# The last 48 inner rows of each routed expert enter the down product as stacked rounded parts

## The reference, cut to what matters

```python
w_topk, sel = jax.lax.top_k(probs, K)          # K = 4 of E = 32 experts
buf = buf[:, :CAP]                             # CAP = 128 token slots an expert, H = 256
g = jnp.einsum('ech,ehf->ecf', buf, w_gate)    # F = 176 inner rows
u = jnp.einsum('ech,ehf->ecf', buf, w_up)
y = jnp.einsum('ecf,efh->ech', jax.nn.silu(g) * u, w_down)
```

## Time and profile before

| | |
|---|---|
| median of 3 runs | 700.69 us (700.65 to 703.05) |
| the profiled execution's own time | 701.29 us |
| its span, first to last instruction | 699.1 us |
| TensorE busy | 671.0 us (96%) |
| VectorE busy | 489.0 us (70%) |
| ScalarE busy | 424.3 us (61%) |
| GpSimd busy | 297.8 us (43%) |
| chain that ended last | PE 76%, DVE 14%, ACT 6%, issue 3% |
| granted clock of TensorE | 1.00 throughout |

### The profile page before, as it was taken

How to read it: one execution, slowest core, us unless ns; L and a number is a source line. 1 busy time by engine, 2 the same in 40 slices (tenths; PEclk the granted TensorE clock), 3 DMA queues, 4 the chain that set the end, 5 groups by cost and what they waited for, 6 DMA issues and landing times.

```text
span 699.1 us, 13847 instructions
## 1 busy us (share of the span) xinstructions
PE 671.0 (96%) x4756; PEld 581.7 (83%) x4756; DVE 489.0 (70%) x1418; ACT 424.3 (61%) x1099; POOL 297.8 (43%) x301
## 2 busy tenths in 40 slices
PE   6999999999999999999999989999989999999997
PEld 3777888888889898887787855666889999999997
DVE  6798877877877787777786886777465555644544
ACT  3766168788797878888663788888654213222221
POOL 0584154546464555542164318998334410400000
PEclk9999999999999999999999999999999999999999
DMA  8902044453535444351910000200300000000000
GB/s 329 346 1 98 1 130 121 165 166 112 168 116 165 129 152 126 101 159 59 365 79 1 1 1 2 107 1 3 121 1 1 1 1 16 2 16 1 1 16 16
DMA packets 26725, 59.43 MB, mean 85 GB/s; under 512 B 3146, under 2 KB 12748, under 8 KB 26272
## 3 DMA queue, kind: packets, MB, share of 16 engines
q1 hardware_dynamic: 23584, 50.35, 21.5%
q0 software_dynamic: 3072, 8.20, 3.6%
HBM read 48.24 MB, written 10.49 MB: 84 GB/s over the span
## 4 chain that ended last, share of the span: by engine, by line
PE 76%; DVE 14%; ACT 6%; issue 3%; POOL 1%; DMA 0%; DVEq 0%; ACTq 0%
PE bank L2253 11%; PE bank L2020 7%; PE bank L1954 6%; PE bank L2302 5%; PE bank L2011 5%; PE bank L2276 5%; PE bank L2040 4%; PE bank L1961 3%; PE bank L2031 3%; PE bank L2082 3%; PE bank L2316 2%; PE bank L2222 2%; PE bank L2206 2%; PE bank L1894 2%; PE bank L2161 2%
## 5 line engine op out<-in xcount | busy, mean ns | idle before, releaser
L1062 ACT ACTIVATE sb<-bank,sb 128x256 f32<-128x256 f32 x128 | 59.6, 471 | 40.6 <-DVE sb L1558 33.4
L1558 DVE TENSOR_REDUCE sb<-bank 128x2 f32<-128x512 f32 x64 | 43.7, 683 | 47.5 <-PE bank L2020 47.1
L1264 ACT ACTIVATE h_parts<-sb 128x256 fp32r<-128x256 f32 x56 | 23.4, 418 | 71.3 <-DVE sb L1809 43.4
L2020 PE MATMUL bank<-sb 128*128 128x256 f32 x256 | 66.2, 381 | 0.0
L1800 DVE TENSOR_TENSOR sb<-sb,bank 128x256 f32<-128x256 f32 x56 | 23.5, 419 | 58.1 <-ACT sb L1227 58.1
L2253 PE MATMUL bank<-rounded,b_hi 128*128 128x256 f32 x224 | 63.1, 282 | 0.0
L2253 PE MATMUL bank<-rounded,b_lo 128*128 128x256 f32 x224 | 62.9, 281 | 0.0
L2253 PE MATMUL bank<-am_lo,b_hi 128*128 128x256 f32 x224 | 62.9, 281 | 0.0
L1227 ACT ACTIVATE sb<-bank 128x256 f32<-128x256 f32 x56 | 21.5, 383 | 62.4 <-PE bank L2253 62.4
L834 POOL DMA_INDIRECT expert_out<-sb x32 | 33.0, 1032 | 61.0 <-DVE sb L1500 44.6
L1069 ACT ACTIVATE sb<-sb 128x256 f32<-128x256 f32 x128 | 57.7, 503 | 0.1
(11 more groups left out here) (321 smaller groups left out, 1969.9 us busy)
## 6 DMA issues: line engine op xcount, KB each, us to landing
sb<-in_w_gate_up SPq DMA_DIRECT2D x32, 368.0 KB
sb<-in_w_down SPq DMA_DIRECT2D x32, 256.0 KB
sb<-in_w_pair SPq DMA_DIRECT2D x8, 704.0 KB
expert_out<-sb SPq DMA_DIRECT2D x1, 4096.0 KB, 23.7
sb<-expert_out SPq DMA_DIRECT2D x8, 512.0 KB, 6.3
sb<-in_w SPq DMA_DIRECT2D x1, 1792.0 KB, 13.8
sb<-in_b SPq DMA_DIRECT2D x1, 1792.0 KB, 8.1
sb<-in_sw_up SPq DMA_DIRECT2D x1, 1536.0 KB, 9.4
```

The costliest lines, as they stand in the source:

```text
L1062: act.activation(probs[:, u % 4, q, :], bank[3 + u % 2][:, q * S:(q + 1) * S], ACT.Exp, scale=-1.0, bias=row_min[:, u % 4, q:q + 1], accum ...
L1558: dve.tensor_reduce(row_min[:, u % 4, :], bank[3 + u % 2][:, :].rearrange("p (q n) -> p q n", q=QT), AX.X, ALU.min).then_inc(at_min, 1)
L2020: mm = pe.matmul(bank[3 + u % 2][:, q * S:(q + 1) * S], qb[i][:, h, b * S + q * P:b * S + (q + 1) * P], keys[:, h, b * S:(b + 1) * S], sta ...
```

## The change

The inner rows 128 to 175 of an expert's hidden values are kept as two parts, a rounded one in partitions 0 to 47 and the rest in partitions 64 to 111 of one new tile, `e_rest`, whose other partitions are zero. The down weights of these rows are now stored twice, at the same partitions, and are split into a rounded high part `w_dn_hi` (ScalarE) and a low part `w_dn_lo` (GpSimd, written over the raw weights). The second f32 product of the down product becomes two fp32r products, of `e_rest` with the high and with the low weights. VectorE makes one product more and a subtraction for each expert. ScalarE's part is put two places ahead of the expert's turn and GpSimd's one place ahead; the down product itself comes one turn later. TensorE's turn now waits for VectorE's products through `ex_gu`, and the down product for the subtraction through `ex_h`. The weight tile has the size it had.

```diff
+REST_HIGH, REST_LOW = ({at - sooner: e for at, e in EXPERT_TURN.items() if e < E0} for sooner in (2, 1))
...
-W_SPLITS = SU_STEPS
+LO_AT = UP_AT
+DN_AT = [SETS * KD * GU + 2 * D * s + D for s in range(SETS)]
+KV_TOK_AT = 2 * (2 * 2 * P + 2 * 3 * KVL + 2 * D) + 2 * TOK
+W_SPLITS = SU_STEPS + E0
...
+    wd = f["L0_ffn_w_down"]
+    gap = np.zeros((E0, UP_AT - FR, D), np.float32)
+    out["w_down"] = np.concatenate([wd, gap, wd[:, P:], gap], 1).reshape(E0, 2, P, D).transpose(0, 2, 1, 3)
...
+            def rest_low(e, s):
+                pool.wait_ge(w_high, SU_STEPS + e + 1)
+                pool.tensor_tensor(r(w_dn_lo[s][:, :]), w_dn[s][:, 1, :], w_dn_hi[:, s, :], ALU.subtract).then_inc(w_low, 1)
...
                     for place in range(PLACES):
+                        e = REST_LOW.get(place_of_unit(p, u, place))
+                        if e is not None:
+                            rest_low(e, e % SETS)
                         e = EXPERT_GATE.get(place_of_unit(p, u, place))
...
+            def rest_high(e, s, before):
+                if e == 0:
+                    act.wait_ge(at_v, 4)
+                act.wait_ge(ed_in[s], 16 * before + 16)
+                act.activation(r(w_dn_hi[:, s, :]), w_dn[s][:, 1, :], ACT.Copy).then_inc(w_high, 1)
+
             def experts(p, u, place):
+                e = REST_HIGH.get(place_of_unit(p, u, place))
+                if e is not None:
+                    rest_high(e, e % SETS, e // SETS)
                 e = EXPERT_TANH.get(place_of_unit(p, u, place))
...
                 dve.scalar_tensor_tensor(e_gu[:, s], e_act[:, s], 1.0, gates, ALU.add, ALU.mult).then_inc(ex_gu, 1)
-                dve.wait_ge(ex_gu, e + 1)
-                dve.scalar_tensor_tensor(e_hid[:, s, 0], e_gu[:, s, 0], 0.5, bank[1][:, 2 * P:3 * P], ALU.mult, ALU.mult)
-                dve.scalar_tensor_tensor(e_hid[0:FR, s, 1], e_gu[0:FR, s, 1], 0.5, bank[1][UP_AT:UP_AT + FR, P:2 * P],
-                                         ALU.mult, ALU.mult).then_inc(ex_h, 1)
+                dve.wait_ge(ex_gu, 4 * e + 1)
+                rest_gate, rest_up = e_gu[0:FR, s, 1], bank[1][UP_AT:UP_AT + FR, P:2 * P]
+                dve.scalar_tensor_tensor(e_hid[0:FR, s, 1], rest_gate, 0.5, rest_up, ALU.mult, ALU.mult).then_inc(ex_gu, 1)
+                dve.scalar_tensor_tensor(r(e_rest[0:FR, s]), rest_gate, 0.5, rest_up, ALU.mult, ALU.mult).then_inc(ex_gu, 1)
+                dve.scalar_tensor_tensor(e_hid[:, s, 0], e_gu[:, s, 0], 0.5, bank[1][:, 2 * P:3 * P], ALU.mult, ALU.mult)\
+                    .then_inc(ex_gu, 1)
+                dve.wait_ge(ex_gu, 4 * e + 4)
+                dve.tensor_tensor(r(e_rest[LO_AT:LO_AT + FR, s]), e_hid[0:FR, s, 1], e_rest[0:FR, s], ALU.subtract).then_inc(ex_h, 1)
...
                 if i == HALF:
+                    dve.wait_ge(at_v, 3)
+                    dve.memset(e_rest, 0.0).then_inc(at_v, 1)
                     effective_qk(0, 0, bank[4])
...
             def down(e, s, before):
-                pe.wait_ge(ed_in[s], 16 * before + 16)
-                for f in range(2):
-                    mm = pe.matmul(bank[1][:, KD * P:KD * P + D], e_hid[:, s, f, :], w_dn[s][:, f, :],
-                                   start=(f == 0), stop=(f == 1))
-                mm.then_inc(ex_done, 1)
+                dst = bank[1][:, KD * P:KD * P + D]
+                pe.wait_ge(w_low, SU_STEPS + e + 1)
+                pe.wait_ge(ex_h, e + 1)
+                pe.matmul(dst, e_hid[:, s, 0, :], w_dn[s][:, 0, :], start=True, stop=False)
+                pe.matmul(dst, r(e_rest[:, s, :]), r(w_dn_hi[:, s, :]), start=False, stop=False)
+                pe.matmul(dst, r(e_rest[:, s, :]), r(w_dn_lo[s][:, :]), start=False, stop=True).then_inc(ex_done, 1)
...
                     if e:
-                        pe.wait_ge(ex_h, e)
+                        pe.wait_ge(ex_gu, 4 * e)
```

More of the change, by code:

```diff
@@ L238, in lay_out @@
     out["w_gate_up"] = gu.reshape(E0, KD, P, GU).transpose(0, 2, 1, 3)
-    out["w_down"] = np.concatenate([f["L0_ffn_w_down"], np.zeros((E0, 2 * P - F0, D), np.float32)],
-                                   1).reshape(E0, 2, P, D).transpose(0, 2, 1, 3)
+    wd = f["L0_ffn_w_down"]
+    gap = np.zeros((E0, UP_AT - FR, D), np.float32)
+    out["w_down"] = np.concatenate([wd, gap, wd[:, P:], gap], 1).reshape(E0, 2, P, D).transpose(0, 2, 1, 3)
     out["w_qkvg"] = tiles(np.concatenate([f["L1_attn_Wq"], f["L1_attn_Wk"], f["L1_attn_Wv"], f["L1_ffn_Wg"]]).T)
@@ L330, in program @@
             su_lo = over("su_lo", start[1] + SU_AT, KD * 2 * NF * P)
+            w_dn_lo = []
+            w_dn_lo.append(over("w_dn_lo0", start[2] + DN_AT[0], D))
+            w_dn_lo.append(over("w_dn_lo1", start[2] + DN_AT[1], D))
             su_hi = over("su_hi", start[2] + SU_HI_AT, KD * 2 * NF * P)
+            w_dn_hi = over("w_dn_hi", start[3] + KV_TOK_AT, SETS * D)
+            e_rest = over("e_rest", start[3] + KV_TOK_AT + SETS * D, SETS * P)
         with ExitStack() as overlay:
@@ L446, in program @@
         w_dn = [r3.take(2, D) for _ in range(SETS)]
+        w_dn_hi = w_dn_hi[:, :].rearrange("p (s n) -> p s n", s=SETS)
+        e_rest = e_rest[:, :].rearrange("p (s n) -> p s n", s=SETS)
         xe = r3.take(SETS, D)
@@ L464, in program @@
         keys = r4.take(2, TOK)
+        assert r4.at == KV_TOK_AT
         kv_tok = r4.take(NT, 3 * KVL)
@@ L1522, in experts @@
                     if e == 0:
-                        dve.wait_ge(at_v, 1)
+                        dve.wait_ge(at_v, 4)
                     hidden(e, e % SETS)
```

## The result

| | before | after |
|---|---|---|
| median of 5 runs each, measured together | 700.87 us (700.65 to 703.05) | 712.61 us (711.23 to 713.16) |
| profiled execution, its span | 701.29, 699.1 us | 711.23, 709.4 us |

What follows compares the result with a forecast made beforehand. TensorE (99% busy) bounds the stretch on the whole, but VectorE's list sets the handovers. 5.50 (five pairs) + 0.88 (first) + 0.56 (seventh) + 2.33 (last six) + 0.50 (copy) = 9.8 us, giving median 710.5, range 703.5 to 714.5.

Steps and rivals of the forecast that it cites:

- The mechanism and the pair time: VectorE's list sets the gate-product handovers; a pair gets 0.22 + 0.34 + 0.54 = 1.10 us longer, from 30.9 to 32.0.
- the late projection ahead of unit 5: Merged queries on ScalarE come 0.54 us later, delaying TensorE's projection; 0.34 us remains at unit 5's gate product.
- The added VectorE work: Between two minima: product 0.31 us plus subtraction 0.23 (0.10 to 0.35), together 0.54 us (0.41 to 0.66).
- TensorE's saving: Down product takes 0.67 us, freeing 0.20 an expert, 6.4 in all; a gain only where TensorE ends last.
- Five pairs and the seventh: Handovers of five whole pairs cost 5.50 us, those of the seventh, up to the closer spacing, 0.56.
- First pair: The first pair, with fewer experts, costs 0.34 + 0.54 = 0.88 us.
- the one that kept the subtraction's meeting with GpSimd out of the sum: VectorE's subtraction beside GpSimd's SBUF work: up to 0.4 us in six pairs, 2.4 us, counted only in the range.
- the one that costed GpSimd's subtraction at nothing: GpSimd's low weights, 0.8 us each, lie in its idle half and add nothing; readers of work behind come later.
- rival (d): Shared port adds 2.4 us, or late down weights delay softmax: +13 to +16, 714 to 717 us; chance 0.10.
- Close spacing: The last six handovers cost 2.33 us, and ScalarE's new copy ahead of tanh 0.50 once.
- (b): Units 1, 3, 5 have more room, or VectorE's pieces vanish; TensorE's saving comes through, 694.3 us in full; chance 0.07.
- (c): A wash: product and subtraction overlap, only 0.2 to 0.3 us reaches handovers; 702 to 704.5 us; chance 0.13.

Runs made afterwards that it cites:

- m1: Changed kernel with ScalarE copying the merged queries ahead of its expert piece in units 4 and 6; 712.32 us, 1.0159 to the kernel before.
- e4: Changed kernel without VectorE's subtraction and the down product's wait for it, both products kept; 699.88 us, 0.9977 to the kernel before.
- e1: Changed kernel without VectorE's second product and subtraction, TensorE's shorter down product kept; 698.88 us, 0.9964 to the kernel before.
- c1: Changed kernel with VectorE's two copies ahead of the row minimum where no query rotation stands there (units 1 and 7); 715.89 us, 1.0213 to the kernel before.
- s1: Changed kernel with VectorE's subtraction moved behind the low parts, only the rounded down products waiting for it; 715.28 us, 1.0209 to the kernel before.
- c5: Changed kernel with VectorE's copies ahead of the minimum in all odd units and merged queries earlier on ScalarE; 732.03 us, 1.0445 to the kernel before.

## Why the prediction was right, by its own steps

**The mechanism and the pair time: right.** Pair 1.10 us longer predicted, 1.07 measured in the undisturbed pairs. The interval ahead of unit 7 grew by 0.50 (0.54 predicted), that of unit 1 by 0.35, that of unit 3 by 0.14, that of unit 5 by 0.08, together 0.57, against my 0.22, 0 and 0.34, together 0.56. The single terms were wrong, and that their sum was right is partly luck. The 0.12 us that a waiting load gives back falls into the interval behind it, which I had booked at the load itself, and the late projection ahead of unit 5, for which I had 0.34, costs next to nothing: m1 takes it away and the row copy is there to be waited for.

**The added VectorE work: the sum was right, its parts were not.** 0.56 us was measured for 0.54. I had 0.31 for the product and 0.23 for the subtraction; by e4 it is 0.12 and 0.44. The product costs little because it stands behind one with the same starts; the subtraction is long because it waits, starts elsewhere and holds the next one. The bound of 0.35 that I gave it from the nearest row was too low. Nothing in the time showed this, only e4 did.

**TensorE's saving: right.** 0.67 for the down product; e1 shows that even with an unchanged list on VectorE only about a third of the 6.4 us comes through (701.06 to 698.88).

**The sum.** Five pairs and the seventh: 6.06 predicted; the lag of the gate loads behind those of the kernel before grew from 1.6 us at the fourth gate load (116.56 against 114.93) to 7.9 at the load at 301.71 (293.79 before), 6.3. First pair: 0.88 predicted, 2.0 measured. The steps that failed are two at the same place: the one that kept the subtraction's meeting with GpSimd out of the sum, and the one that costed GpSimd's subtraction at nothing and did not see it stand behind the rope split at expert 0. VectorE's subtraction took 1.1 us more there and TensorE waited 1.28 us for the low weights; beside that the two met only at 225.02 and 242.09 (0.49 and 0.43 us). The Trainium skill (SBUF — State Buffer, Who interferes with whom) has it that a VectorE instruction with two SBUF inputs contends with a GpSimd instruction that reads SBUF, and by it, the trace agrees; but rival (d), 0.4 us in every pair, did not come. Close spacing: 2.33 + 0.50 predicted, from a lag of 7.9 to the span's 10.3: 2.4. The down weights were not late (0.4 us in two waits). Together 9.8 predicted and 10.3 measured between the spans: 2.0, 6.3 and 2.4, less 0.4 by which the first gate load came sooner (92.69 against 93.07). Why it came sooner is open. That the whole is so close is partly luck: the first pair's 1.1 us more stand against 0.4 less at the close and 0.4 less at the start.

**The median.** The profiled executions differ by 9.9 us (711.23 - 701.29), the medians by 11.7; I had set the median 0.6 below the profile's own time, and for the kernel after it lies 1.4 above it. This is nearly all of the 2.1 us by which 710.5 missed.

**The rivals.** (b), TensorE's saving comes through, falls: pair 32.0, not 30.1. (c), a wash by overlap in VectorE's pipeline, falls for the change as made; the overlap exists for the second product, and e4 (699.88) is what the change gives with that alone; it does not for the subtraction.

## What to carry to other kernels

Where an engine at 77% hands work back to one at 99%, measure the room at each handover and add new work to the list between two of them, not to the engine's total: 0.56 us an expert, four experts a pair, cost 1.1 us a pair here while the busier engine was relieved of 0.8. Price a short VectorE instruction by the distance to its neighbours, with the partition at which each operand starts, and keep instructions of one start together. Before moving work, ask what it makes late for the other engines and what it will newly run beside: c1 and s1 lost about 3 us more than the change itself, c5 19, by a late minimum or late rotated queries and by a subtraction that then met GpSimd.

## What the runs showed of the hardware

- On VectorE the start of the next short instruction comes 0.20 to 0.21 us behind one of 0.29 us if all operands start at the same partitions, and 0.30 to 0.32 us if one starts at 64 instead of 0 or back; for long ones it is 0.61 and 0.70 behind 0.67 to 0.69. A semaphore from the instruction just in front costs the same as a changed start (0.31).
- 112 partitions took no longer than 48 (0.28 to 0.29 us).
- A VectorE subtraction with both inputs in SBUF that met GpSimd's SBUF work did not slow down by a share: nearly everywhere it ended 0.14 to 0.16 us behind GpSimd's instruction. At expert 0 it ended behind the last of three in a row (1.38 us for 0.28). At 225.02 it ended 0.15 us behind an addition of the rope split, although GpSimd's next instruction had begun.
